# Graph-network kernel: the last layer's products, norm and stores moved into its sum, and x loaded in 25 pieces

## The reference, cut to what matters

```python
x = layernorm(x + gcn(x))          # two neighbour sums, symmetric norm
x = layernorm(x + gated(x))        # sums over in- and out-edges, GRU cell
x = layernorm(x + edge_mlp(x))     # sums of 64 edge features per node, 3-layer MLP
# last layer (L3), with inv_deg = 1 / max(in-degree, 1):
h   = relu(x @ Ws0 + (segment_sum(x[src], dst) * inv_deg) @ Wn0 + b0)   # 256 wide
out = h @ Ws1 + (segment_sum(h[src], dst) * inv_deg) @ Wn1 + b1         # 128 wide
x = layernorm(x + out)
```

## Time and profile before

| | us |
|---|---|
| runs | 1045.37, 1044.33, 1043.19 (median 1044.33) |
| profiled execution, whole | 1042.22 |
| its span, first to last instruction | 1040.5 |
| PE busy / DVE busy / ACT busy | 940.3 / 625.4 / 477.6 |

### The profile page before, as it was taken

How to read it: one execution, slowest core, us unless ns; L and a number is a source line. 1 busy time by engine, 2 the same in 40 slices (tenths; PEclk the granted TensorE clock), 3 DMA queues, 4 the chain that set the end, 5 groups by cost and what they waited for, 6 DMA issues and landing times.

```text
span 1040.5 us, 19510 instructions
## 1 busy us (share of the span) xinstructions
PE 940.3 (90%) x7324; PEld 823.0 (79%) x7324; DVE 625.4 (60%) x951; ACT 477.6 (46%) x767; POOL 60.0 (6%) x133
## 2 busy tenths in 40 slices
PE   7559999999689999969989989989999799999992
PEld 6459999999689979969988878845445599879982
DVE  3759999999354465575564445445564755315544
ACT  0225444445556556656647757622633433343312
POOL 1200000000000000000002324300000000000000
PEclk9979999999899999989999989989999899999997
DMA  9668777776100000000000000000000000000001
GB/s 283 135 141 177 166 166 166 165 167 129 30 1 0 1 1 0 0 16 0 0 1 1 0 1 0 0 1 1 11 0 1 20 1 0 1 1 1 0 0 62
DMA packets 168663, 48.01 MB, mean 46 GB/s; under 512 B 154948, under 2 KB 167268, under 8 KB 168593
## 3 DMA queue, kind: packets, MB, share of 16 engines
q1 hardware_dynamic: 155462, 44.96, 18.6%
q10 hardware_dynamic: 12012, 0.83, 0.8%
q0 software_dynamic: 1120, 1.29, 0.5%
HBM read 45.44 MB, written 8.02 MB: 51 GB/s over the span
## 4 chain that ended last, share of the span: by engine, by line
PE 85%; DVE 5%; SPq 3%; ACT 3%; issue 2%; DMA 1%; DVEq 0%; ACTq 0%
PE bank L1506 17%; PE bank L1507 17%; PE bank L1449 11%; PE bank L1439 7%; PE bank L1605 4%; PE bank L1598 4%; PE bank L1606 4%; PE bank L1690 2%; PE bank L1640 2%; PE bank L1411 2%; SPq L477 1%; PE bank L1698 1%; PE bank L1641 1%; PE bank L1679 1%; PE bank L1678 1%
## 5 line engine op out<-in xcount | busy, mean ns | idle before, releaser
L1506 PE MATMUL bank<-stage,f_hi 125*128 125x392 f32 x1000 | 345.5, 346 | 15.6 <-DVE f_lo L1136 10.6
L1507 PE MATMUL bank<-stage,f_lo 125*128 125x392 f32 x1000 | 343.1, 343 | 0.0
L1019 DVE CAST stage<-counts 125x2352 fp32r<-125x2352 uint8 (+1 forms) x120 | 165.5, 1382 | 84.7 <-PE bank L1507 84.6
L1506 PEld LDWEIGHTS bank<-stage,f_hi 125*128 125x128 f32 x1000 | 190.2, 190 | 18.2 <-issue 14.6
L1507 PEld LDWEIGHTS bank<-stage,f_lo 125*128 125x128 f32 x1000 | 190.1, 190 | 0.0
L711 ACT ACTIVATE stage<-counts 125x1568 fp32r (+1 forms) x80 | 107.7, 1346 | 177.1 <-PE bank L1507 174.1
L1449 PE MATMUL bank<-tmp,wb 128*65 128x25 f32 x2000 | 130.8, 220 | 10.8 <-DVE tmp L971 10.8
L1449 PEld LDWEIGHTS bank<-tmp,wb 128*65 128x65 f32 x2000 | 127.7, 143 | 11.0 <-DVE tmp L971 11.0
L657 ACT ACTIVATE counts<-bank 125x500 uint8<-125x500 f32 x188 | 87.0, 536 | 43.4 <-PE bank L1439 42.9
L798 ACT ACTIVATE stage<-bank 125x500 fp32r<-125x500 bf16 x150 | 87.5, 588 | 38.0 <-PE bank L1598 26.8
L948 DVE TENSOR_TENSOR xT<-xT,tmp 128x2560 bf16<-128x2560 bf16 (+1 forms) x63 | 92.4, 1467 | 1.2 <-ACT rowb L637 1.2
(11 more groups left out here) (212 smaller groups left out, 940.5 us busy)
## 6 DMA issues: line engine op xcount, KB each, us to landing
wb<-in_edge_attr SPq DMA_DIRECT2D x125, 256.0 KB, 3.4
lists_d<-in_dst SPq DMA_DIRECT2D x1, 3104.0 KB
lists_d<-in_src SPq DMA_DIRECT2D x1, 3104.0 KB
...
xT<-in_dst SPq DMA_DIRECT2D x63, 4.0 KB, 3.0
xT<-in_dst ACTq DMA_DIRECT2D x62, 4.0 KB, 3.0
...
```

The costliest lines, as they stand in the source:

```text
L1019: nc.vector.tensor_copy(set_buffer(u, m), counts[:, SETS[u][0]:sum(SETS[u]), chunk(pair * 2 + off)]).then_inc(s["set_d_ready"], 1)
L1506: mm(bank[h][:, 0:CH], f_hi[:, first + k, :], rhs[:, k, :], start=(first + k == 0), stop=False)
L1507: last = mm(bank[h][:, 0:CH], f_lo[:, first + k, :], rhs[:, k, :], start=False, stop=(first + k == HI - 1))
```

## The change

1. *x.* The one transfer behind piece 5 is gone. Instead SP issues one tile (125 partitions of 512 bytes) behind every third piece from e = 36 on, 25 transfers up to e = 108. PE waits for all of them where it waited for the one.
2. *Fifth sum.* PE's, ACT's and DVE's loops over chunks are written out for this sum. PE makes the own-feature products of chunk 0 ahead of the sum and those of chunk c+1 inside chunk c, before its fourth set; behind them, still before the fourth set, it transposes the group whose last chunk is c-1 (groups 0 to 4 in chunks 2, 3, 4, 6 and 7). DVE adds products, bias and xT into `wa` (`own_part`) before the keep of the chunk; the keep goes to `tmp`, and `result` adds it to `wa`. The add of xT by itself (L1374) is gone. Statistics of groups 0 to 4 stand inside the sum.
3. *Norm and stores.* Three parts instead of two (groups 0-2, 3-4, 5-6). DVE and ACT do parts 0 and 1 between their widenings, all but the last steps of part 1; ACT scales groups 0 to 4 and 6, DVE group 5. The scaled groups go to three rotating places in `wl1`, as `wb` is still read by the products; from group 3 on the scaling waits for the store of the group three before, and the stores count on three semaphores.
4. The code of the general path for this layer moves behind the end, and gets its own norm.

What does not change: the number of products, transposes and statistics, the widenings, and the bytes loaded and stored.

The diff, cut to its core:

```diff
-                if e == RE - 1:
-                    sp.dma_start(wa[:LO, :].rearrange("p (h f) -> p h f", h=HI), x.rearrange("(h l) f -> l h f", l=LO)).then_inc(s["x_in"], 16)
+                if e >= X_FROM and (e - X_FROM) % 3 == 0 and (e - X_FROM) // 3 < HI:
+                    h = (e - X_FROM) // 3
+                    sp.dma_start(wa[:LO, h * D:(h + 1) * D], x[h * LO:(h + 1) * LO, :]).then_inc(s["x_in"], 16)
...
-        PARTS_OF = ((0, 2, NGR), (0, 3, 5, NGR), (0, 3, 5, NGR), (0, 4, NGR))
-        ACT_SCALES = ((0, 1, 2, 3), (0, 1, 2), (3, 4), (0, 2, 4, 6))
+        PARTS_OF = ((0, 2, NGR), (0, 3, 5, NGR), (0, 3, 5, NGR), (0, 3, 5, NGR))
+        ACT_SCALES = ((0, 1, 2, 3), (0, 1, 2), (3, 4), (0, 1, 2, 3, 4, 6))
...
+            if i == 3:
+                return wl1[:LO, 512 * (k % 3):512 * (k % 3) + n * D].rearrange("p (h f) -> p h f", h=n)
...
-                sp.dma_start(out[g * LO:(g + n) * LO, :].rearrange("(p q) f -> p (q f)", q=n), wb[:LO, g * D:(g + n) * D]).then_inc(s["out_done"], 16)
-            sp.wait_ge(s["out_done"], 16 * NGR)
+                sp.dma_start(rows_of_out(k), z_group(3, k).rearrange("p h f -> p (h f)")).then_inc(out_done[k % 3], 16)
+            for k in (4, 5, 6):
+                wait_stored(sp, k)
...
-            neighbour_sum(4)
-            deviations(3, 0)
-            scaled(3, 0)
+            for pair in range(NC // 2):
+                for h in range(2):
+                    for u in (1, 3):
+                        widen_set(4, pair, h, u)
+                    if pair * 2 + h == 4:
+                        deviations(3, 0)
+                    if pair * 2 + h in (5, 6):
+                        scaled(3, pair * 2 + h - 5)
...
+            def own_part(c):
+                dve.wait_ge(s["l3_y"], c + 1)
+                nc.vector.scalar_tensor_tensor(wa[:, chunk(c)], bank[2 + c % 2][:, 0:CH], cols[:, C_L3B1:C_L3B1 + 1], xT[:, chunk(c)],
+                                               ALU.add, ALU.add).then_inc(s["pre_made"], 1)
+                for k in range(5):
+                    if chunks_for[k] == c:
+                        statistics(3, k)
+                if c == 4:
+                    variances(3, 0)
+                if c == 5:
+                    scales(3, 0)
+                if c == 7:
+                    variances(3, 1)
+                    scales(3, 1)
+                dve.wait_ge(s["pre_made"], c + 1)
...
+            neighbour_sum(4, lambda c: tmp[:, 1 + c % 2, :], result, unrolled=True, early=own_part)
...
-            pe.wait_ge(s["x_in"], 16)
+            pe.wait_ge(s["x_in"], 16 * HI)
...
+            def between(c):
+                if c + 1 < NC:
+                    if c >= 1:
+                        pe.wait_ge(s["pre_made"], c)
+                    own_state(2 + (c + 1) % 2, c + 1).then_inc(s["l3_y"], 1)
+                for k in range(5):
+                    if chunks_for[k] == c:
+                        node_group(3, k, "y_made", 2 * NC + chunks_for[k])
+            own_state(2, 0).then_inc(s["l3_y"], 1)
+            for c in range(NC):
+                sum_chunk(4, c // 2, c % 2, between)
+            for k in (5, 6):
+                node_group(3, k, "y_made", 3 * NC)
```

More of the change, by code:

```diff
@@ L220, in gnn_program @@
         g_rows_in = [sem(f"g_rows_in{k}") for k in range(8)]
+        out_done = [sem(f"out_done{b}") for b in range(3)]
         list_in = [sem(f"list_in{q}") for q in range(NQ)]
@@ L880, in _ @@
             upper_halves(4)
-            neighbour_sum(4)
-            deviations(3, 0)
-            scaled(3, 0)
+            for pair in range(NC // 2):
[6 more added lines that the diff above has]
+                        scaled(3, pair * 2 + h - 5)
             scaled(3, 2)
             deviations(3, 1)
+            scaled(3, 3)
             scaled(3, 4)
+            deviations(3, 2)
             scaled(3, 6)
+            taken = flag_of(act)
+            with act.If(taken):
+                act.wait_ge(s["g_redo"], R_NODES + 4)
+                nc.scalar.activation(n_whole("sd"), n_whole("var"), ACT.Sqrt, bias=cols[:LO, C_EPS:C_EPS + 1], scale=1.0 / D).then_inc(s["g_redo"], 1)
         @block.vector
@@ L1385, in _ @@
-            for k in range(counted, 4):
-                statistics(3, k)
-            variances(3, 0)
-            statistics(3, 4)
-            scales(3, 0)
-            scaled(3, 1)
+                nc.vector.scalar_tensor_tensor(wa[:, chunk(c)], bank[2 + c % 2][:, 0:CH], cols[:, C_L3B1:C_L3B1 + 1], xT[:, chunk(c)],
[3 more added lines that the diff above has]
+                        statistics(3, k)
@@ new lines, in own_part, with result @@
+                if c == 4:
[6 more added lines that the diff above has]
+                dve.wait_ge(s["pre_made"], c + 1)
+            def result(c):
+                nc.vector.tensor_tensor(wa[:, chunk(c)], wa[:, chunk(c)], tmp[:, 1 + c % 2, :], ALU.add).then_inc(s["y_made"], 1)
+            neighbour_sum(4, lambda c: tmp[:, 1 + c % 2, :], result, unrolled=True, early=own_part)
@@ L1486, in _, with sum_chunk @@
             general_products(pe, 0, taken, [("xt_kept", NGR), ("fold_kept", 2), ("bias_kept", 1)])
+            def sum_chunk(q, t, h, between=None):
+                for u, (first, n) in enumerate(SETS):
+                    if u % 2 == 0:
+                        m = h * 3 + u // 2
+                        pe.wait_ge(s["set_d_ready"], t * 6 + (24 * q + m + 1))
+                    else:
+                        m = h * 2 + u // 2
+                        pe.wait_ge(s["set_a_ready"], t * 4 + (16 * q + m + 1))
+                    if h == 0:
+                        pe.wait_ge(s["f_lo_made"], q * NGR + (first + n - 1) // 4 + 1)
+                    if u == 0:
+                        wait_bank(q, t, h)
+                    if u == 3 and between is not None:
+                        between(t * 2 + h)
+                    rhs = set_buffer(u, m)
+                    for k in range(n):
+                        mm(bank[h][:, 0:CH], f_hi[:, first + k, :], rhs[:, k, :], start=(first + k == 0), stop=False)
+                        last = mm(bank[h][:, 0:CH], f_lo[:, first + k, :], rhs[:, k, :], start=False, stop=(first + k == HI - 1))
+                    last.then_inc(s["set_a_used"] if u % 2 else s["set_d_used"], 1)
             def neighbour_sum(q):
```

127 lines of the change are left out of this document (76 added, 51 removed).

## The result

| | before | after | change |
|---|---|---|---|
| median of the runs, us | 1043.76 (4 runs, 1040.47 to 1045.37) | 1028.73 (4 runs, 1027.17 to 1037.3) | ratio 0.9881, 95% 0.9835 to 0.9928 |
| profiled execution, us | 1042.22 | 1037.3 | |
| its span, us | 1040.5 | 1035.6 | -4.9 |
| mean granted clock of the span | 0.960 | 0.956 | |

The kernel is faster, by some 15 us in the medians, where 20.2 were forecast: 1028.7 against 1024.1. It also scatters more than the kernel before, and the time goes roughly with the granted clock: in the four runs and two further ones it is 1037.3 us at 0.956, 1033.5 at 0.961, 1029.5 at 0.966, 1027.2 at 0.967, and 1030.3 and 1028.0 at 0.969. The median of the six is 1029.9.

A forecast was written before the change was run, and what follows sets the result against it. DVE's pace and its wait behind x in the first stage, and the fifth sum's end, were taken as bounds on PE; 11.2 + 9.0 = 20.2 us won, tiles costing 0, gave 1024.1 us, likeliest 1021 to 1027, wider range 1019 to 1031.

The forecast's parts named there:

- likeliest case: Whole kernel: the forecast of 1024.1 us with its own range of 1021 to 1027, chance 0.78.
- both places: First stage, where DVE paces PE and once waits 11.22 us; and the end, 35.35 us from the last keep.
- The stop: First stage: DVE waits 11.22 us for the targets of pieces 6 and 7, held in SP's queue behind x.
- rival C: First stage: the 11.22 us wait isn't x's, rings may be full of earlier pieces; only 9.0 won, 1035.3; chance 0.05.
- rival B: Fifth sum: PE waits in chunks for ACT or DVE, 8 to 12 us back, 1034 in the middle; chance 0.05.
- Part 2: Fifth sum and end: work moved ahead of the last keep and a shorter end win 9.0 us.
- nearly met: End, ACT: group 6's wait at T + 4.9 (T: last keep's start) for group 3's store, done near T + 4.8.
- SP's branch: End: SP branches over the general path behind its wait, costing 0.7 us, bounds 0 and 1.4.
- Part 1: First stage: without x behind piece 5, DVE's wait for targets goes, which gives 11.2 us.
- What the 25 tiles cost: 0: First stage: SP lacks 2.2 us for the tile issues, but pieces have 4.8 us in hand, so no cost.
- Rival A: First stage: the tiles hold the edge pieces; all 14.8 us back gives 1038.9, half 1031.5; chance 0.08.
- upper bound of 14.8: First stage: most the 25 tiles could cost, 0.59 us of SP's time a tile, 14.8 us in all.

The follow-up runs named there:

- part 2 alone: The changed kernel with x as one transfer behind piece 5, as before the change: 1035.37 us, ratio 0.9911 to the kernel before.
- part 1 alone: The kernel before with only x changed, to 25 tiles issued by SP behind every third piece from e = 36: 1044.56 us, ratio 1.0010.

## Why the prediction was right in part and wrong in its sum

*The number.* 1028.7 lies above the 1021 to 1027 of the likeliest case and inside the wide range of 1019 to 1031. That it lies inside was in part luck: the same kernel on the second chip has 1034.1, above 1031.

*What bounds the kernel*: both places were read rightly. The stop was x's (part 2 alone keeps it, and it is gone where x is), so rival C falls; there is no gap in the fifth sum, so rival B falls.

*Part 2, forecast 9.0*: right. From the first `f_lo` to the last keep it took 14.6 us longer, forecast 15.1; from the last keep to the end 11.7, forecast 11.3; 35.35 - 14.6 - 11.7 = 9.0. Chunks lasted 10.25 and 11.05, forecast 10.3 and 11.0. The stored-wait of group 6 cost ACT 0.52 us off the path, as "nearly met" had it. SP's branch, taken at 0.7, doesn't show: the last data moved before 1035.0, and the span ends at 1035.6. The last stores ran slower than taken instead.

*Part 1, what it gives, forecast 11.2*: a little too much. The kernel before with the tiles from ACT's queue gained 9.2. The term was read from one trace, in which DVE came to the stop early. The stop's end was fixed by x, its beginning wasn't.

*"What the 25 tiles cost: 0"*: this is the step that failed. They cost 9.5 us in the kernel before (ratio 1.0010 with SP's queue, 0.9919 with ACT's), and in the changed kernel 4.3 to 9.7 (1028.7 and 1034.1 against 1024.4). The prediction's own sum showed SP's queue 2.2 us short, and it was set aside because pieces have 4.8 us in hand. Three things were wrong in that.

First, a tile costs SP 0.76 us and not 0.59: the gaps around an issue belong to its price. Then the tiles need 19 us of SP against 12.6 of slack, and SP is 6.4 us short, not 2.2. Slack is also what makes up for an issue that is held; with none left, each of them stays. Second, the lead was measured at the wrong engine. The 8.2 us run from the issue to PE, which reads the features; DVE asks for the targets 6.46 us after their issue, so with 3.4 us to land 3.1 were in hand, 1.6 with the longest landing of 4.9. The trace has SP 3.2 us behind when the first wait comes. This correction needed only rows of the kernel before, SP's and DVE's side by side. Third, the price of running out was taken as the wait itself, when it was the wait and then 14 us of PE at half its clock.

The first wait of over 0.5 us for targets ends at 172.99, 173.81 and 174.71 us in the three traces with whole tiles in SP's queue, as a lead that is used up at an even pace would have it. Rival A had the place right, with SP's slack short, and in its lower half (1031.5) about the size; I gave it 0.08. In the kernel before with part 1 alone the whole gain went (1.0010), so there the upper bound of 14.8 was nearer than 0.

With the tiles in ACT's queue the rest of the sum is whole: 9.2 + 9.0 = 18.2, and measured -19.0 (1043.39 to 1024.4).

The Trainium skill, "DMA: Bandwidth & Descriptors", section "Bandwidth", says to batch DMAs to 1 MiB and more. Here fewer issues did help (13 transfers were 7.7 us better than 25), but the largest one was worst: a single 1.6 MB transfer over few engines stopped the stage in both places where it stood among the pieces, 9.1 us behind piece 5 and 16.68 in step 15, and behind the last piece PE waited 13.47 us for it. The 2.0 us of fixed time that the prediction takes from that page stand there for DMAs issued by GpSimd, and these are SP's; nothing in the argument hangs on them.

What stays open: no run tells what holds an issue. How many drops of the clock a run has differs (two in the trace of the changed kernel, one in that of the kernel before with part 1 alone), and with it the time. And a gap is not always followed by one: in that last trace a wait of 1.46 us for targets at 226.76 was not, the granted clock is 1.00 from 200 to 262 us. All later traces have DVE's first pair at 38.2 to 40.6 us and only that of before at 37.15; whether the kernel before starts so as a rule isn't known. And of the 5 us between the changed kernel on the two chips (1028.7 and 1034.1; the intervals of the ratios overlap) how much is the chip's and how much the scatter of runs.
